# Latent attention rebuilt: scores made in both directions, no transposes, operand stacks loaded for four heads at a time

## What is computed

```python
q, k, v = x @ Wq, x @ Wk, x @ Wv
latent_kv = (k + v) @ W_down_kv
k_rec, v_rec = latent_kv @ W_up_k, latent_kv @ W_up_v       # 16 heads of 16 channels
scores = einsum('bhqd,bhkd->bhqk', qh, kh) / 16
scores = clip(scores, -10000, 10000)
scores = scores * exp(-0.0001 * abs(i - j))                 # i query, j key
scores = clip(scores, -10000, 10000)
out = softmax(scores) @ vh
```

## Time and profile before

| | us |
|---|---|
| median of 3 runs | 1612.59 (1612.44 to 1614.67) |
| profiled execution | 1615.76 |
| its span | 1614.2 |
| latent_projections, in the span | 22.69 to 83.99 |
| latent_attention, first matmul to next block's | 90.91 to 622.23 |

### The profile page before, as it was taken

The page is one execution under the profiler, slowest core; times in us unless marked ns, Lnnn a source line. Parts: engine busy times, 40 slices in busy tenths (PEclk is TensorE's granted clock), DMA queues, the critical chain, the costliest instruction groups (busy, mean ns, idle before and its releaser), DMA issues. The chain is left out here.

```text
span 1614.2 us, 36474 instructions
## 1 busy us (share of the span) xinstructions
PE 1340.0 (83%) x12288; PEld 960.2 (59%) x12291; DVE 919.8 (57%) x2059; ACT 930.1 (58%) x1793; POOL 190.5 (12%) x546
## 2 busy tenths in 40 slices
PE   5879999999999995898365699889874489999992
PEld 2347777777777774544223464364354279999992
DVE  5558888888888873532788844563354223323233
ACT  2469999999999991355375377624631033333330
POOL 0001111111111110111200000031120701111110
PEclk9879999999999997899756899988995589999996
DMA  3311010010101013200000100033006211111115
GB/s 115 131 51 31 22 27 24 24 26 23 29 20 29 20 38 110 80 1 4 16 1 0 31 1 1 1 120 129 1 4 212 102 34 36 37 36 38 36 33 166
DMA packets 60025, 74.30 MB, mean 46 GB/s; under 512 B 13006, under 2 KB 47728, under 8 KB 59952
## 3 DMA queue, kind: packets, MB, share of 16 engines
q1 hardware_dynamic: 53168, 56.76, 11.9%
q0 software_dynamic: 4672, 14.50, 2.7%
q10 hardware_dynamic: 2112, 2.10, 0.4%
HBM read 50.43 MB, written 22.88 MB: 45 GB/s over the span
## 5 line engine op out<-in xcount | busy, mean ns | idle before, releaser
L659 DVE CUSTOM_DVE_ANT_0 probs_sb<-banks,decay_sb 128x1024 f32<-128x1024 f32 x256 | 308.2, 1221 | 43.6 <-PE banks L578 22.5
L706 ACT ACTIVATE probs_sb<-probs_sb,shift_sb 128x1024 f32<-128x1024 f32 x256 | 294.8, 1151 | 18.1 <-POOL shift_sb L563 16.4
L588 PEld LDWEIGHTS banks<-ident_sb,probs_sb 128*128 128x128 f32 x2048 | 238.3, 141 | 55.1 <-issue 22.9
L588 PE MATMUL banks<-ident_sb,probs_sb 128*128 128x128 f32 x2048 | 267.8, 274 | 0.9 <-ACT probs_t_sb L521 0.8
L521 ACT ACTIVATE probs_t_sb<-banks 128x512 f32<-128x512 f32 x384 | 214.7, 597 | 4.1 <-PE banks L588 2.3
L578 PE MATMUL banks<-k_stack_sb,q_stack_sb 96*128 96x512 bf16 x512 | 156.9, 389 | 14.0 <-DMA k_stack_sb<-k_parts 10.7
L603 PE MATMUL banks<-probs_t_sb,v_head_sb 128*32 128x128 f32 x4096 | 151.2, 277 | 0.7 <-ACT probs_t_sb L521 0.7
L1846 PEld LDWEIGHTS banks<-slots_xt_sb,tile_w_sb 128*128 128x128 f32 x1248 | 146.5, 193 | 1.9
L1846 PE MATMUL banks<-slots_xt_sb,tile_w_sb 128*128 128x128 f32 x1248 | 146.6, 276 | 0.0
L1858 PE MATMUL banks<-experts_w_sb,xt_sb 128*128 x624 | 141.2, 379 | 1.3 <-issue 1.3
L1892 ACT ACTIVATE slots_xt_sb<-banks 128x256 f32<-128x256 f32 x39 | 14.9, 383 | 213.8 <-PE banks L1832 213.8
(11 more groups left out here) (289 smaller groups left out, 1910.0 us busy)
## 6 DMA issues: line engine op xcount, KB each, us to landing
experts_w_sb<-in_L_ffn_W SPq DMA_DIRECT2D x16, 1024.0 KB, 11.9
q_stack_sb<-q_parts SPq DMA_DIRECT2D x192, 32.0 KB, 1.7
k_stack_sb<-k_parts SPq DMA_DIRECT2D x192, 32.0 KB, 1.8
slots_x<-zeros_sb POOLq DMA_DIRECT2D x1, 5031.0 KB, 22.6
slots_x_sb<-slots_x SPq DMA_DIRECT2D x39, 129.0 KB, 2.1
xt_sb<-outputs_y SPq DMA_DIRECT2D x8, 512.0 KB, 5.5
q_parts<-parts_sb SPq DMA_DIRECT2D x8, 384.0 KB, 3.0
k_parts<-parts_sb SPq DMA_DIRECT2D x8, 384.0 KB, 4.2
```

Source lines behind the costliest of these rows:

```text
L588: last = pe.transpose(k.ps[:, 4 + half, j * P:(j + 1) * P], pr[:, s % 4, (half * TPG + j) * P:(half * TPG + j + 1) * P], k.ident[:, :])
L659: dve.tensor_tensor_reduce(out=pr[:, s % 4, :], in0=scores, in1=decay[:, off:off + S], scale=1.0, scalar=-3.0e38, op0=ALU.mult, op1=ALU.ma ...
L706: act.activation(pr[:, s % 4, :], pr[:, s % 4, :], ACT.Exp, bias=shift[:, s % 8:s % 8 + 1], accum_out=sums[:, (s // TPG) % 4, s % 4:s % 4 ...
```

## The change

**Decay in the operands.** exp(-c|i-j|) is exp(-ci) exp(cj) for keys before the query and the reverse for keys after it. The projections now write two faded versions of each piece (32 instead of 16): DVE multiplies by a fade table and takes the extremes, DVE subtracts the first part, and POOL (idle there before) subtracts the second. 32 stores of 384 KB go out; after the 21st to 26th, the stacks of the first group are loaded between them.

**Scores twice.** The work goes in 16 groups of four heads x 512 queries. For each of a group's 16 tiles PE makes the scores with queries on partitions as before, now only for the maximum, which DVE takes (a table is still multiplied in, for the diagonal block). The maxima are split in three parts by POOL, turned by PE, copied by ACT, and sent by SP into three more rows of the query stack, against rows of the key stack that hold -1. PE then makes the scores a second time with keys on partitions; they come out with the maximum already subtracted, and ACT takes the exponential of 128 x 512 straight from PSUM. Nothing is transposed, and PE sums the values of four heads side by side over 512 columns. A column of ones among the values gives the sum. On the diagonal both versions are made; POOL zeroes one triangle of each (affine_select). The maxima run one group and six tiles ahead.

**Loads.** One transfer now carries both versions of four heads: 16 partitions x 2 x 8 KB for keys (256 KB), 16 x 2 x 4 KB for queries (128 KB). An even group needs six of each (2.36 MB), an odd group the six of queries (0.79 MB). They are asked for when the group two before starts. Rows of Wq and W_up_k are put in another order ahead of time so that the 16 partitions are the 16 channels.

**Clip path.** The path for scores that reach the bound is rewritten too; the bound of the flag is lowered. It does not run with this data.

```diff
-def latent_projections(k, v_heads, q_scratch, k_scratch):
+def latent_projections(k, v_heads, fade_in, stacks, later):
...
@@ -374,38 +387,54 @@
...
+            def apply_fade(e):
+                n, version = divmod(e, 2)
+                dve.wait_ge(qk_ready, n + 1)
+                wait(dve, part3_done, e - 3)
+                side = version if is_query(e) else 1 - version
+                half = n // 4 % 2
+                sign = 1.0 - 2.0 * version
+                dve.nop(nofuse=True)
+                dve.tensor_tensor_reduce(out=rest[:, e % 4, :], in0=k.ps[:, n % 4, :], in1=fade[:, side, half * G:(half + 1) * G],
+                                         scale=sign * (scale if is_query(e) else 1.0), scalar=-3.0e38, op0=ALU.mult, op1=ALU.max,
+                                         accum_out=extremes[:, version, n:n + 1]).then_inc(faded, 1)
+
...
+            def subtract_first(e):
+                dve.wait_ge(part1_done, e + 1)
+                dve.tensor_tensor(rest[:, e % 4, :], rest[:, e % 4, :], parts[:, e % SLOTS, 0, :],
+                                  ALU.subtract).then_inc(rest1_done, 1)
...
-            own.wait()
+            own.did(dve.tensor_scalar(k.inside[:, :], bound[:, :], 0.9 * CLAMP / HD * float(np.exp(-2.0 * DECAY * S)), None, ALU.is_lt))
+            own.wait()
+
+        @block.gpsimd
+        def _(pool):
+            for e in range(NV):
+                pool.wait_ge(part2_done, e + 1)
+                pool.wait_ge(rest1_done, e + 1)
+                pool.tensor_tensor(parts[:, e % SLOTS, 2, :], rest[:, e % 4, :], parts[:, e % SLOTS, 1, :],
+                                   ALU.subtract).then_inc(part3_done, 1)
...
         def _(sp):
-            for n in range(NP):
+            for v in range(2):
+                sp.dma_start(fade[:, v, :], fade_in[v].partition_broadcast(P)).then_inc(fade_arrived, 16)
+            later.start(sp)
+            for e in range(NV):
...
-
+                scratch = stacks.q_scratch if s < 2 else stacks.k_scratch
+                sp.wait_ge(part3_done, e + 1)
+                rows = slice(b * D + m * P, b * D + (m + 1) * P)
+                sp.dma_start(scratch[version, :, half, rows, :].rearrange("c p n -> p c n") if s < 2 else
+                             scratch[version, :, rows, half * G:(half + 1) * G].rearrange("c p n -> p c n"),
+                             parts[:, e % SLOTS, :, :]).then_inc(stored[e % SLOTS], 16)
+                if e == 19:
+                    for x in range(SLOTS):
+                        sp.wait_ge(stored[x], 16 * len(range(x, 16, SLOTS)))
+                if 20 <= e < 26:
+                    load_stacks(sp, stacks, 0, e - 20)
+            for x in range(SLOTS):
+                sp.wait_ge(stored[x], 16 * len(range(x, NV, SLOTS)))
+            later.wait(sp)
...
+def load_stacks(eng, stacks, g, piece):
+
+    n, half = divmod(g, 2)
+    b, first = divmod(n * HEADS, H)
+    rows = slice(b * D + first * HD, b * D + (first + HEADS) * HD)
+    q_part, k_part = [(0, 0), (0, 1), (0, 2), (1, 0), (1, 1), (2, 0)][piece]
+    dst = slice(piece * HD, (piece + 1) * HD)
+    if half == 0:
+        eng.dma_start(stacks.k[dst, n % 2, :, :, :].rearrange("p v h n -> p v (h n)"),
+                      stacks.k_scratch[:, k_part, rows, :].rearrange("v (p h) n -> p v (h n)", h=HEADS)
+                      ).then_inc(stacks.arrived[g % 3], 16)
+    eng.dma_start(stacks.q[dst, g % 3, :, :, :].rearrange("p v h n -> p v (h n)"),
+                  stacks.q_scratch[:, q_part, half, rows, :].rearrange("v (p h) n -> p v (h n)", h=HEADS)
+                  ).then_inc(stacks.arrived[g % 3], 16)
+
...
-            bodies(sp, body)
+            def store_peaks(g):
+                sp.wait_ge(peaks_copied, g + 1)
+                sp.dma_start(stacks.q[ROWS:ROWS + PARTS, g % 3, :, :, :].rearrange("p v h n -> p (v h n)"),
+                             peak_rows[:, g % 2, :]).then_inc(peaks_in, 16)
+
+            for g in range(1, 3):
+                for piece in range(6):
+                    load_stacks(sp, stacks, g, piece)
+            store_peaks(0)
+            for g in range(1, GROUPS):
+                store_peaks(g)
+                if g + 2 < GROUPS:
+                    sp.wait_ge(key_scored, g * UNITS)
+                    for piece in range(6):
+                        load_stacks(sp, stacks, g + 2, piece)
+
...
+            def key_product(g, i, h, bank, version, lo, hi, at):
+                kt = key_tile(g, i)
+                return pe.matmul(k.ps[:, bank, at:at + hi - lo],
+                                 stacks.k[0:ROWS + PARTS, g // 2 % 2, version, h, kt * P:(kt + 1) * P],
+                                 stacks.q[0:ROWS + PARTS, g % 3, version, h, lo:hi], start=True, stop=True)
...
+            def sum_values(s):
+
+                g, i = divmod(s, QT)
+                n, kt = g // 2, key_tile(g, i)
+                pe.wait_ge(exp_done, unit_index(g, i, HEADS if on_diagonal(i) else HEADS - 1) + 1)
+                if i == 0:
+                    pe.wait_ge(v_staged, n + 1)
+                    wait(pe, mix_copied, g)
+                if on_diagonal(i):
+                    pe.wait_ge(selected, s // 2 + 1)
+                    lo = block_of(g, i) * P
+                    for h in range(HEADS):
+                        pe.matmul(k.ps[VW * h:VW * (h + 1), PV_BANK, lo:lo + P], vh[:, n % 2, h, kt, :],
+                                  probs_d[:, s // 2 % 2, h, :], start=False, stop=False, skip_group_check=True)
+                for h in range(HEADS):
+                    last = pe.matmul(k.ps[VW * h:VW * (h + 1), PV_BANK, :], vh[:, n % 2, h, kt, :], probs_of(s)[:, h, :],
+                                     start=i == 0, stop=i == QT - 1, skip_group_check=True)
+                last.then_inc(summed, 1)
...
+            pe.wait_ge(constants, 2)
+            for tile in range(TILES + LEAD):
+                scores(tile)
+                if tile == TILES + 1:
+                    turn_peaks(0)
...
+            own.did(pool.memset(vh[:, :, :, :, :], 0.0))
+            own.wait()
+            pool.memset(stacks.k[ROWS:ROWS + PARTS, :, :, :, :], -1.0).then_inc(constants, 1)
+            pool.wait_ge(constants, 1)
+            pool.tensor_copy(ident_b[:, :], k.ident[:, :]).then_inc(constants, 1)
+            pool.wait_ge(constants, 2)
+            own.did(pool.memset(vh[:, :, :, :, HD:HD + 1], 1.0))
...
+            def select(g, i):
+                s = g * QT + i
+                lo = block_of(g, i) * P
+                later = probs_of(s)[:, :, lo:lo + P]
+                pool.wait_ge(exp_done, unit_index(g, i, HEADS - 1) + 1)
+                pool.affine_select(later, later, [[0, HEADS], [1, P]], ALU.is_ge, 0.0, base=0, channel_multiplier=-1)
+                earlier = probs_d[:, s // 2 % 2, :, :]
+                pool.wait_ge(exp_done, unit_index(g, i, HEADS) + 1)
+                pool.affine_select(earlier, earlier, [[0, HEADS], [-1, P]], ALU.is_gt, 0.0, base=0,
+                                   channel_multiplier=1).then_inc(selected, 1)
+
...
+            def highest(tile):
+                g, x = divmod(tile, TILES)
+                dve.wait_ge(scored, tile + 1)
+                wait(dve, peaks_split, g - 1)
+                wait(dve, peaked, tile - 1)
                 dve.nop(nofuse=True)
-                dve.tensor_tensor_reduce(out=pr[:, s % 4, :], in0=scores, in1=decay[:, off:off + S],
+                dve.tensor_tensor_reduce(out=junk[:, tile % 2, :], in0=tile_scores(tile), in1=inner[:, window(tile)],
                                          scale=1.0, scalar=-3.0e38, op0=ALU.mult, op1=ALU.max,
-                                         accum_out=peak[:, s % 8:s % 8 + 1]).then_inc(peaked, 1)
-
...
+            def exponential(g, i, h):
+                u, s = unit_index(g, i, h), g * QT + i
+                act.wait_ge(key_scored, u + 1)
+                act.wait_ge(released, u + 1)
+                if h == 0:
+                    wait(act, summed, s - 2)
+                if h < HEADS:
+                    out = probs_of(s)[:, h, :]
+                else:
+                    wait(act, summed, s - 3)
+                    out = probs_d[:, s // 2 % 2, :, :].rearrange("p h n -> p (h n)")
+                act.activation(out, k.ps[:, bank_of((exp_done, u + 1)), :], ACT.Exp).then_inc(exp_done, 1)
+
...
@@ -2149,6 +2382,13 @@
     a["c_numbers"] = np.ascontiguousarray((SLOT_TILES * P + np.arange(T, dtype=np.float32)).reshape(NT, P).T)
     a["c_before"] = np.triu(np.ones((P, P), np.float32), 1)
     width = (2 * QT - 1) * P
+    by_channel = np.arange(D).reshape(H // HEADS, HEADS, HD).transpose(0, 2, 1).reshape(D)
+    for name in ("L0_attn_Wq", "L0_attn_W_up_k"):
+        a[name] = np.ascontiguousarray(a[name][:, by_channel])
+    ahead = np.arange(width)[None, :] - (QT - 1) * P - np.arange(P)[:, None]
+    own_tile = (np.arange(width)[None, :] >= (QT - 1) * P) & (np.arange(width)[None, :] < QT * P)
```

(67 more changed lines are left out.)

547 lines of the change are left out of this document (286 added, 261 removed).

## The result

The changed kernel takes **1629.67 us** (median of 4 runs, 1625.72 to 1632.95) against 1612.51 us (1611.95 to 1614.67) for the kernel before: a ratio of 1.0103, 95% interval 1.0077 to 1.0129. It is slower, by about 1%. The forecast was 1624 us, 5.7 us less, with slower as the likelier side. The profiled execution is 1628.12 us long, with a span of 1626.0 us.

What follows compares the result with a forecast made beforehand. PE was to bound the steady work, with waits for loads. Projections +22.6, start +14.4, attention -29 and end +2.8 made +11 on 1612.6: 1624 us; eight in ten 1553 to 1655.

Steps and rivals of the forecast that it cites:

- What bounds the steady work: Attention's steady groups: PE becomes the bound at 25.5 us a group, against ACT 20.2 and DVE 20.3 plus 0.7.
- The rival in which TensorE is not the bound: Steady work: matmuls overlap better, ACT and DVE leave 23 us a group, up to 35 us less, 1590 us; chance 0.06.
- The loads: Stack loads at 107 GB/s: PE waits 6.8 us in six even groups, plus 2 us each for the clock; 53 us.
- The rival with fast loads: Stack loads at 200 GB/s and more: no waits, projections end at 94 us, kernel takes 1558 us; chance 0.28.
- The argument for fast loads: Stack loads: at 66 GB/s the engines are held 0.27 of the time, so they have room for more.
- The projections: Stage before attention: 1.6 us a version, 21st store issued at 68 us, block ends at 106.6 us; +22.6 us.
- three engines near 1.4 that hand to each other: Projections: ACT, DVE and POOL each need near 1.4 us a version, so 1.6 us was taken.
- the DMA term: Projections, behind the 21st store: 12 stores and 2.36 MB of loads (22 us) until 104 us, 2.6 us to land.
- The blocked engines: Projections: DVE's and POOL's subtractions may not overlap, a version costs 2.0 us, everything shifts 13 us, 1637 us; chance 0.14.
- The start: Start of the attention block: PE waits for POOL's memsets, the bf16 one 17.7 us; first scores after 21.3 us, +14.4 us.
- The end: End of the attention block: the scratch clear follows POOL's last selects and holds the next block back; +2.8 us.
- The selects: POOL's affine_selects on the diagonal, taken at 0.85 us; rival: at 1.3 us PE waits 43 us, 1667 us; chance 0.08.

Runs made afterwards that it cites:

- Experiment 5: Changed kernel with the 16 rows of a piece going to every sixth of the 96 partitions instead of 16 neighbours; 1578.44 us.
- Experiment 1: Changed kernel with TensorE making a group's two query pieces before the values of the group before, not behind them; 1623.48 us.
- Experiment 2: Changed kernel with TensorE waiting for GpSimd's constants only before the first turn of the maxima, not before the first scores; 1613.95 us.

## Why the prediction was right, and where it was off

- **What bounds the steady work** was right. TensorE, 26.0 us a group instead of the forecast 25.5, ScalarE 19.2 and VectorE 19.7 instead of 20.2 and 21.0. The rival in which TensorE is not the bound is out. The sizes were too small: some 6 us over groups 1 to 12, and 5.8 from group 13 on: at the end ScalarE alone was to decide, and it waited for TensorE as well. That -27.0 came so near to -29 is in part luck, for the loads had been priced 10 us too high.
- **The loads** were right in mechanism, place and number: six waits at the sixth step of the even groups. The rate was 114 GB/s where 107 had been taken from bursts of small transfers; an even group's stacks were there after 22.6 us (24.1 forecast) and wanted after 17.8 (17.3). A wait was 5.1 us on average instead of 6.8. The half clock behind it cost 2.1 us, as taken. In all 43 us instead of 53. Experiment 5 confirms both the 43 us and the cause. The rule of the Trainium skill cited against the change (SBUF — State Buffer, Door 1: The DMA port swizzle) pointed the right way; its 104 GB/s at 1 MiB are 114 here, at 128 and 256 KB. The rival with fast loads had a wrong price: experiment 5 has 231 GB/s and takes 1578.4 us, not 1558. The loads were worth 51 us, not 66, and the other errors stay.
- **The argument for fast loads**, that the engines had been little used at 66 GB/s, misled. They show a share of 1.01 at 114 GB/s in the trace of after, and 1.01 at 231 in experiment 5: the share says how long packets are under way, not how much an engine could still carry. With a share of 1.01 at 114 GB/s an engine moves 7.1 GB/s, half of the 15 that the trace of before had shown; that trace has no stretch in which loads to 16 partitions fill the engines.
- **The projections** are the step that failed, in size: +29.4 us instead of +22.6. The 1.6 us a version was right where nothing is missing (1.57). But the 21st store came at 79.5 and not at 68, because "three engines near 1.4 that hand to each other" left TensorE out. Its order puts the values of the last group, whose copies stand behind ScalarE's pieces, ahead of the queries of the next. The 21st store was so 11.5 us late. Experiment 1 gives 6.0 back for the order; the two waits for the latent values that remain in it make 5.1 more. From the 21st store to the end it took 33.8 us; forecast were 38.6, so the DMA term was too long, and the two errors partly cancel.
- **The blocked engines**, the rival at 2.0 us a version, did not come true, but half of it is real: next to each other VectorE's subtraction takes 1.03 instead of 0.69 us and GpSimd's 1.60 instead of 1.15. Strict turns would have made 0.69 + 1.15 = 1.84 us a version at least (1.76 with the 0.61 that lie between two starts on VectorE alone), above the 1.57 measured. The Trainium skill (SBUF — State Buffer, Who interferes with whom), cited for this rival, calls the shared port an exclusive lock; the contention shows here, a lock for the whole instruction does not.
- **The start**: the wait for the memset was right; it took 13.75 us, not 17.7. That is 0.84 ns for each bf16 element, the bound worked out from an f32 memset. The row of the same type, a memset of 1178 ns for 1024 elements, was the worse guide. Experiment 2 shows that the wait can be avoided: 15.7 us came back.
- **The end** was right in mechanism; the clear landed 1.8 us sooner after its issue than its row of before (20.8 against 22.6), which is most of the difference between +0.7 and +2.8.
- **The selects** take 0.64 us each, not 0.85; only one wait of 1.0 us on TensorE comes from them. The rival is out.
- The errors of the terms (+6.8, -4.0, +2.0, -2.1, -1.7) come to +1.0 against the measured span. That the sum was near 11 owes something to that.

## What to carry to other kernels

Before a large operand is gathered by rows, look at the partitions that one transfer writes: the same bytes over the same queue ran at 114 GB/s to 16 neighbours and at 231 to every sixth partition, with nothing else changed. When the loops of a transfer are rearranged for that, keep a factor of 16 outermost, or few engines carry it (76 GB/s). And follow a wait to what is really read behind it: the memset, the clear and the values each held up work that did not need them, for 16, 16 and 6 us.

## What the runs showed that had not been expected

- A DMA engine's share of 1.01 went with 114, 159, 231 and, in the stores, 333 GB/s. Full engines are no sign of a full rate.
- A transfer to more partitions can be slower: 76 GB/s at a share of 0.21 with the loop over 3 or 2 pieces outermost, where 16 neighbours had 114; with the sixteen outermost it was 159.
- The subtractions of VectorE and GpSimd stretch each other by 0.34 and 0.45 us without taking strict turns.
- TensorE's granted clock stood at 0.50 until about 236 us after the wait that ended at 231.06, although TensorE worked without a gap; it was at 1.00 before the wait.
